# Exponentials of a decoder stack: 32x32 block transposes on VectorE and moves by DMA in place of TensorE transposes

## The reference, cut to what matters

```python
x = x + att0                    # attention 0: batch 0 alone, one result added to all batches
x = mamba_block(x)              # projection, causal 4-tap convolution, scan over 8 heads, gate
x = x + cross_attention(ln(x))  # attention 1: 8 heads of 32, padding mask
x = ln(x + mha_causal(x))       # attention 2: 16 heads of 16
x = ln(x + mha(x, context))     # attention 3: 16 heads of 16
x = ln(x + fc2(relu(fc1(x))))
x = ln(x + mha_causal(x, ctx))  # attention 4: 16 heads of 16
x = x + down(gelu(up(x)))
```

## Time and profile before

| what | us |
|---|---|
| median of 3 runs | 1736.97 |
| lowest, highest run | 1736.25, 1737.17 |
| span of the profiled execution | 1734.3 |
| TensorE busy in it | 1664.1 |
| ScalarE busy | 1357.1 |
| VectorE busy | 1313.4 |
| GpSimd busy | 533.5 |

### The profile page before, as it was taken

One profiled execution on the slowest core, in us unless ns is written; L12 is line 12 of the kernel. 1 busy time (PEld: TensorE's weight loads), 2 busy tenths in 40 slices (PEclk: granted clock), 3 DMA queues, 4 the chain that ended last, 5 costly groups with the idle time before them and its releaser, 6 DMA issues.

```text
span 1734.3 us, 54906 instructions
## 1 busy us (share of the span) xinstructions
PE 1664.1 (96%) x21232; PEld 1438.0 (83%) x21232; DVE 1313.4 (76%) x3355; ACT 1357.1 (78%) x4026; POOL 533.5 (31%) x1288
## 2 busy tenths in 40 slices
PE   6789999999999999999999999999999999999976
PEld 6577888888888888888888888888888888888765
DVE  3577778887778888877888887788888778888542
ACT  2367888888888888888888888888888888888763
POOL 1333233332323333232333333233333323333110
PEclk9899999999999999999999999999999999999998
DMA  7000000000000000000000000000000000000000
GB/s 266 8 8 8 8 8 12 6 10 9 11 12 11 11 6 10 9 11 11 12 11 8 8 8 11 12 11 11 10 5 9 10 11 11 9 5 5 5 4 10
DMA packets 26176, 26.92 MB, mean 16 GB/s; under 512 B 2240, under 2 KB 25024, under 8 KB 25792
## 3 DMA queue, kind: packets, MB, share of 16 engines
q1 hardware_dynamic: 25920, 23.41, 4.1%
HBM read 19.21 MB, written 4.19 MB: 13 GB/s over the span
## 4 chain that ended last, share of the span: by engine, by line
PE 88%; DVE 7%; issue 2%; ACT 1%; POOL 1%; DMA 0%; DVEq 0%; SPq 0%; POOLq 0%; ACTq 0%
PE ring L581 26%; PE ring L587 22%; PE ring L569 18%; PE score L637 6%; PE ring L678 5%; PE ring L755 3%; PE ring L765 2%; DVE conv L1237 2%; PE ring L668 2%; PE ring L816 1%; DVE conv L1231 1%; PE score L628 1%; DVE neg_max L1144 1%; PE ring L748 1%; ACT exps L954 1%
## 5 line engine op out<-in xcount | busy, mean ns | idle before, releaser
L954 ACT ACTIVATE exps<-score,neg_max 128x128 f32<-128x128 f32 x1808 | 491.4, 409 | 112.7 <-DVE neg_max L1144 112.7
L1144 DVE TENSOR_REDUCE neg_max<-score 128x4 f32<-128x512 f32 x452 | 289.8, 683 | 118.9 <-PE score L637 118.8
L1400 POOL TENSOR_TENSOR stat<-stat 128x1 f32<-128x1 f32 x224 | 128.8, 575 | 698.3 <-DVE stat L1116 698.3
L960 ACT COPY weights<-ring 128x512 f32<-128x512 f32 x452 | 257.3, 658 | 44.0 <-PE ring L569 42.3
L569 PE MATMUL ring<-const,exps 128*128 128x128 f32 x1808 | 240.1, 275 | 11.6 <-ACT exps L954 7.9
L569 PEld LDWEIGHTS ring<-const,exps 128*128 128x128 f32 x1808 | 210.2, 142 | 33.9 <-ACT exps L954 15.8
L1231 DVE SCALAR_TENSOR_TENSOR conv<-raw,vectors,conv 128x128 f32<-128x128 f32 x576 | 168.5, 348 | 6.8
L581 PE MATMUL ring<-actT,w_q 128*128 128x128 f32 x1024 | 138.0, 278 | 2.5 <-ACT actT L926 2.5
L637 PE MATMUL score<-K,QB 32*128 32x128 f32 x3616 | 135.2, 283 | 0.5 <-issue 0.5
L637 PEld LDWEIGHTS score<-K,QB 32*128 32x128 f32 x3616 | 113.8, 188 | 21.9 <-issue 21.7
L926 ACT COPY actT<-ring 128x256 f32<-128x256 f32 x224 | 86.4, 386 | 56.3 <-PE ring L569 56.3
(11 more groups left out here) (165 smaller groups left out, 3472.5 us busy)
## 6 DMA issues: line engine op xcount, KB each, us to landing
cT<-in_ctxT SPq DMA_DIRECT2D x32, 128.0 KB, 2.1
x_in<-in_x SPq DMA_DIRECT2D x32, 128.0 KB, 2.0
out<-result SPq DMA_DIRECT2D x32, 128.0 KB, 2.1
row_all<-in_rows SPq DMA_DIRECT2D x1, 1420.0 KB, 10.2
w_in<-in_in_proj SPq DMA_DIRECT2D x1, 1288.0 KB, 7.2
w_k<-in_k SPq DMA_DIRECT2D x4, 256.0 KB, 6.1
w_v<-in_v SPq DMA_DIRECT2D x4, 256.0 KB, 6.3
w_q<-in_q SPq DMA_DIRECT2D x4, 256.0 KB, 6.8
```

Source lines behind the costliest of these rows:

```text
L954: last = run(exps[:, n, h * P:(h + 1) * P], of, ACT.Exp, bias=neg_max[:, m, h:h + 1])
L960: nc.scalar.copy(weights[:, buffer(it, a_, l, t, WEIGHT_BUFFERS), half * 4 * P:(half + 1) * 4 * P], t_[:, :]).then_inc(read, 1)
L1144: nc.vector.tensor_reduce(neg_max[:, m, 4 * half:4 * half + 4].rearrange("p (b h) -> p b h", b=each), score[:, first:first + each, 0:4 // ...
L1400: tt(stat[:, l, 10:11], stat[:, l, 2:3], stat[:, l, 4:5], ALU.pow).then_inc(S[done], 1)
```

## The change

- No transpose of exponentials is on TensorE any more (BY_PE is empty). ScalarE writes the exponentials of a part in blocks: 4 blocks of (8 heads x 32 keys). One VectorE instruction transposes all 32x32 blocks of the part's 128x1024 in place (`turn_blocks`). Then SP issues 4 DMAs of 128 KB, SBUF to SBUF, one for each quarter of the query partitions; each spreads 32 partitions x 4 runs of 1 KB over 128 partitions of `weights` (`move_blocks`). TensorE's `values` waits for the landing and reads the weights with a stride pattern.
- Column 32 b + i of the scores lands on partition 4 i + b of the weights. So that V can stay as it is, that column holds key 4 i + b: keys, masks and the causal constant are stored in this order, for which ScalarE and VectorE read the key projections from PSUM with a stride of 4 elements.
- `exps` has 3 buffers and not 2. An exponential waits for the move of the part three before; a move waits for the flip and for the reader of the part four before.
- Attention 1's sums come from the exponentials' accumulators; VectorE inverts 8 columns, and TensorE spreads them with as many matmuls as had `ones`. ScalarE copies the outputs (`crossed`) and VectorE multiplies.
- From VectorE to ScalarE: the last tap of the convolution (from PSUM, six Identity activations), xhat, and the row tests (Abs with an accumulator) after x2T and x3T. From VectorE to GpSimd: x1, the gate's product, the additions of epsilon, and the comparisons with zero.
- K1 and V1 have 2 buffers and not 4. The tables TASKS, FIRST, LAST, SETUP and SHIFT are all new; PERIOD is still 14. In the new tables TensorE's list near the third attention reads e3, values1, back4, n3, xbc1, Wo, z0, x2T, x6T, Q2, values3, and VectorE's scores3_1, softplus, turn3_0, down, e3, turn3_1, finish1, finish4, n3, Wo.
- In setup, matmuls that only keep TensorE running stand at other tasks (SPARE), nine of them before values0.

```diff
+BY_PE = ()
 PERIOD = 14
 SCORE_BANKS = 4
-EXPS_BUFFERS = 2
+EXPS_BUFFERS = 3
 MAXIMA_BUFFERS = 4
 WEIGHT_BUFFERS = 4
+BLOCK = P // TILES
...
+            def move_blocks(it, a_, l, t):
+
+                n, _ = turned(it, a_, l, t)
+                part_of = exps[:, buffer(it, a_, l, t, EXPS_BUFFERS), :]
+                sp.wait_ge(S["flipped"], flipped(it, a_, l, t))
+                old = slot_before(it, a_, l, t, WEIGHT_BUFFERS)
+                if old is not None:
+                    was_a, _, was_l, was_i = old
+                    b, use = job(Of(was_i), f"values{was_a}", was_l)
+                    sp.wait_ge(bank_read[b], use + 1)
+                for q, rows_of in enumerate(ROWS_OF):
+                    sp.dma_start(weights[:, n, q * 2 * P:(q + 1) * 2 * P],
+                                 part_of[rows_of].rearrange("i (b x) -> i b x", b=TILES)).then_inc(S[f"turned{n}"], 16)
...
-                    for at, summed in ((D, True), (0, False)):
-                        for c in range(DC):
-                            for r in range(TILES):
-                                h = TILES * c + r
-                                last = mm(output[ROWS_OF[r], at + c * P:at + (c + 1) * P], ones[:, :] if summed else V1[:, l, h, :],
-                                          exps_of(0, heads_of(1, 0).index(h)), start=True, stop=True)
-                                if not summed and c == DC - 1:
-                                    last.then_inc(full if r == TILES - 1 else S[f"att_full{r}"], 1)
+                    pe.wait_ge(S["shares"], nth(it, l))
+                    for c in range(DC):
+                        for r in range(TILES):
+                            h = heads_of(1, 0).index(TILES * c + r)
+                            mm(output[ROWS_OF[r], D + c * P:D + (c + 1) * P], shares[:, l % 2, h:h + 1].broadcast_to((P, DH8)), ident,
+                               start=True, stop=True)
+                    for c in range(DC):
+                        for r in range(TILES):
+                            h = TILES * c + r
+                            last = mm(output[ROWS_OF[r], c * P:(c + 1) * P], V1[:, l % 2, h, :],
+                                      exps_of(0, heads_of(1, 0).index(h)), start=True, stop=True)
+                            if c == DC - 1:
+                                last.then_inc(full if r == TILES - 1 else S[f"att_full{r}"], 1)
...
+                into = exps[:, n, :].rearrange("p (h i b) -> p h b i", h=HEADS, b=TILES) if (a_, t) in BY_PE else exps[
+                    :, n, :].rearrange("p (b h i) -> p h b i", b=TILES, h=HEADS)
+                old = slot_before(it, a_, l, t, EXPS_BUFFERS)
+                if old in STREAMED:
+                    was_a, was_t, was_l, was_i = old
+                    moved, count = turned(Of(was_i), was_a, was_l, was_t)
+                    act.wait_ge(S[f"turned{moved}"], count)
                 for half in range(HALVES):
                     act.wait_ge(S["maxima"], part(it, a_, l, t) * HALVES + half + 1)
                     for h in range(4 * half, 4 * half + 4):
                         of = score[:, 4 * t + h // 2, h % 2 * P:(h % 2 + 1) * P] if a_ == 1 else score[
                             :, 2 * t + h // 4, h % 4 * P:(h % 4 + 1) * P]
-                        last = run(exps[:, n, h * P:(h + 1) * P], of, ACT.Exp, bias=neg_max[:, m, h:h + 1])
+                        if a_ == 1:
+                            last = run(into[:, h], by_block(of), ACT.Exp, bias=neg_max[:, m, h:h + 1], accum_out=sums[:, l % 2, h:h + 1])
+                        else:
+                            last = run(into[:, h], by_block(of), ACT.Exp, bias=neg_max[:, m, h:h + 1])
...
+            def crossed(it, l):
+
+                for r in range(TILES - 1):
+                    act.wait_ge(S[f"att_full{r}"], nth_output(it, 1, l))
+                t, _ = filled(it, "values1", l)
+                nc.scalar.copy(actT[:, l, :, :].rearrange("p c k -> p (c k)"), t[:, 0:D]).then_inc(S["crossed"], 1)
...
+            def xhat(it, l):
+                act.wait_ge(S["rstd1"], nth(it, l))
+                run(att[:, l, :], res[:, l, :], ACT.Copy, scale=stat[:, l, 10:11]).then_inc(S["xhat"], 1)
...
+                               t[:, 0:n * P].rearrange("p (c k) -> p c k", c=n))
+                for k in range(n):
+                    c = half * n + k
+                    last = run(conv[:, l % 2, c, :], t[:, k * P:(k + 1) * P], ACT.Identity,
+                               scale=conv_w[:, c, TAPS - 1:TAPS], bias=conv_b[:, c:c + 1])
+                last.then_inc(read, 1)
...
+            def nonzero_rows(it, what, l, mask, done):
+
+                act.wait_ge(bank_full[job(it, what, l)[0]], job(it, what, l)[1] + 1)
+                run(att[:, l, :], res[:, l, :], ACT.Abs, accum_out=mask[:, l, 0:1]).then_inc(S[done], 1)
+
+            def x2T(it, l):
+                copy_out(it, "x2T", l, actT[:, l], D)
+                nonzero_rows(it, "x2T", l, mask0, "sum0")
+
+            def x3T(it, l):
+                copy_out(it, "x3T", l, actT[:, l], D)
+                nonzero_rows(it, "x3T", l, mask1, "sum1")
...
+            def keys_out(it, what, lane):
+
+                t, read = filled(it, what, lane)
+                for c in range(DC):
+                    last = nc.scalar.copy(by_block(K2[:, lane, c, :]), in_blocks(t[:, c * P:(c + 1) * P]))
+                last.then_inc(read, 1)
...
+            def turn_blocks(it, a_, l, t):
+
+                part_of = exps[:, buffer(it, a_, l, t, EXPS_BUFFERS), :]
+                dve.wait_ge(S["exps"], (part(it, a_, l, t) + 1) * HALVES)
+                nc.vector.transpose(part_of, part_of).then_inc(S["flipped"], 1)
+                if a_ == 1:
+                    nc.vector.reciprocal(shares[:, l % 2, :], sums[:, l % 2, :]).then_inc(S["shares"], 1)
...
-                    for c in chunks:
-                        last = ts(conv[:, l % 2, c, :], raw[:, l % 2, c, TAPS - 1:], conv_w[:, c, TAPS - 1:TAPS],
-                                  conv_b[:, c:c + 1], ALU.mult, ALU.add)
                     for k in range(TAPS - 1):
-                        step(last)
+                        if k:
+                            step(last)
...
+                    heads_out = actT[:, l, :, :].rearrange("p c k -> p (c k)")
+                    tt(heads_out, heads_out, t[:, D:], ALU.mult).then_inc(read, 1)
...
+            def root(it, l, step, seed, done, src=1, scale=1.0, offset=EPS):

                 wait_for(S[seed], nth(it, l))
+                step(ts(stat[:, l, 2:3], stat[:, l, src:src + 1], scale, offset, ALU.mult, ALU.add))
...
+                def x1(l):
+
+                    wait_for(S[f"x_in{l % 2}"], nth_of_two(it, l) * 16)
+                    if it.iteration > 0:
+                        b, use = job(Of(it.iteration - 1), "x6T", l)
+                        wait_for(bank_full[b], use + 1)
+                        wait_for(S["plus"], nth(Of(it.iteration - 1), l))
+                    elif l == 0:
+                        evacuated(it, "back0", 0)
+                    tt(res[:, l, :], x_in[:, l % 2, :], att0[:, :], ALU.add).then_inc(S["x1"], 1)
+
+                def gate(l):
+
+                    wait_for(S["gated"], nth(it, l))
+                    evacuated(it, "Y", l)
+                    m = l % 2
+                    tt(zs[:, m, :], tz[:, m, :], zs[:, m, :], ALU.mult).then_inc(S["u"], 1)
```

More of the change, by code:

```diff
@@ L50 @@
 TASKS = dict(
-    loadx=-39.297, loadc=-21.957, x1=-31.388, x1r=0.609, xhat=34.036, xhatT=-8.817, dt=1.27, softplus=-2.884, am=-12.308,
-    xbc0=-7.003, xbc1=-5.859, z1=-5.461, z0=1.147, K1=-7.656, V1=-0.645, conv0=10.153, conv1=1.914, silu=8.942, pairs=2.154,
-    ld=3.18, decayed=4.453, Y=4.486, uT=5.016, proj=5.731, xnT=7.896, Q1=8.272, finish1=10.278, Wo=13.01, x2T=13.36, K2=15.065,
-    Q2=13.819, V2=18.506, e2=15.211, n2=15.74, finish2=23.561, norm2=19.381, x3T=23.838, row=23.91, K3=24.14, Q3=25.27, V3=24.234,
@@ new lines @@
+    loadx=103.7121, loadc=21.4043, x1=116.7214, x1r=-23.4055, xhat=45.2037, xhatT=101.7706, dt=99.7564, softplus=95.7542,
+    am=54.033, xbc0=104.3449, xbc1=108.5224, z1=106.1759, z0=109.068, K1=104.7433, V1=113.8264, conv0=-120.7388, conv1=-135.3793,
+    silu=69.6664, pairs=112.0066, ld=112.9754, decayed=-70.1916, Y=113.9575, uT=116.0593, proj=116.6788, xnT=118.0147,
+    Q1=118.7217, finish1=121.3722, Wo=123.0545, x2T=123.0968, K2=124.3273, Q2=123.6151, V2=127.245, e2=128.1891, n2=129.6912,
@@ new lines @@
+    finish2=126.3402, norm2=107.8796, x3T=133.292, row=133.8575, K3=133.9645, Q3=133.9878, V3=133.4515, e3=135.9867, n3=136.7537,
+    finish3=218.343, norm3=203.3623, x4T=139.2029, fc1=140.5645, fc2=141.5169, norm4=112.8326, K4=142.6938, V4=146.2533,
+    x5T=143.3817, Q4=144.4216, finish4=178.2296, norm5=189.3358, x6T=151.5575, up0=152.8902, up1=153.0532, down=163.2307,
+    store=263.3565, quads1=119.0754, scores1_0=142.4452, turn1_0=160.0378, values1=122.0848, quads2=125.979, scores2_0=207.3992,
@@ L196 @@
```

(22 more changed lines are left out.)

446 lines of the change are left out of this document (256 added, 190 removed), and 2 rows, old and new, of the table S.

## The result

The changed kernel takes 1855.07 us (median of 4 runs, 1851.48 to 1859.87) against 1736.77 us (1736.25 to 1737.17) for the kernel before beside it: a ratio of 1.068, with a 95% interval of 1.0662 to 1.0698. I had forecast 1588, 9% faster; it is 7% slower.

The account below looks back on a forecast made before the run. TensorE was taken as the only steady bound, busy 96% of 1734.3 us. 1734.3 - 197 (transposes) + 38 (waits) + 10 (setup, drain) = 1585 us of span, 1588 as a run; range 1545 to 1625, chance 0.58.

Parts of the forecast that it names:

- So in the steady part TensorE is the only bound: Steady batches of 50.53 us: TensorE busy 50.33, with ScalarE (83%) and VectorE (81%) running in its shadow.
- What the cover costs: Waits when VectorE is busy 41.9 of 44.4 us: 1.2 us a batch, 38 us; setup and drain add 10 us.
- Rival 3: The change frees nothing: waits refill the time taken off TensorE exactly, 1737 us within 3.5; chance 0.02.
- Rival 1: In-order queues bind: waits of 2.5 to 6 us a batch from late moves or slower VectorE transposes, 1630 to 1733; chance 0.24.
- Rival 2: VectorE takes TensorE's place, slower kernel: a block transpose of 2.5 us or more gives 1754 us or more; chance 0.09.
- Part 1: Transposes taken off TensorE: 226 parts at 0.87 us, 197 us in all, 6.1 us a batch, all on the path.
- Part 2: ScalarE's load: ring copies go (8.0 us a batch), new work adds 7.5; from 42.05 to 41.5 us a batch.
- above 63: Sign of being wrong: table loads above 63; ScalarE would reach 42.8 us with one more in each batch.
- Part 3: VectorE's load: 7.8 us a batch goes, seven block transposes at 1.23 us come; 41.9 us a batch.
- Part 4: GpSimd's load: the gate, x1 and some ten one-column operations add 4.3 us, to 20.8 of 44.4; no bound.
- Part 5: Moves into weights, 904 transfers of 128 KB: 3.7 us from flip to landing; over 5, TensorE waits once a batch.
- The queue: SP's DMA queue: packets took 4.1% of 16 engines' span; the moves add 21% of a 1537 us span; no bound.

Follow-up runs that it names:

- e7: Changed kernel with no turning: ScalarE writes exponentials straight into weights, with no VectorE transposes and no moves; order and small work kept; 1771.33 us, ratio 1.0191.
- e8: Kernel before with no turning: without its 1808 TensorE transposes, ScalarE's 452 copies and 14 spare setup matmuls; own order and small work; 1771.19 us, ratio 1.0191.
- e1: Changed kernel without the moves: VectorE's block transpose writes straight into weights, all else kept; 1803.03 us, ratio 1.037 to the kernel before.
- e9: e8 with other places in each engine's order for some tasks, same work; 1640.67 us, ratio 0.9428 to the kernel before.
- e3: Changed kernel with only the gate's product moved back from GpSimd to VectorE; 1855.36 us, ratio 1.0675 to the kernel before.
- e4: e3 plus the additions of epsilon back on VectorE for five of a batch's seven powers; 1849.22 us, ratio 1.0662 to the kernel before.
- e5: Changed kernel, same instructions, with other places in each engine's order for some tasks; 1898.29 us, ratio 1.0919 to the kernel before.
- e10: Changed kernel, same instructions, with a second new order after e5; 1869.2 us, ratio 1.0748 to the kernel before.
- e12: e8 with 16 more matmuls a batch whose result nobody reads, from the fifth batch on; 1758.01 us, ratio 1.0121 to the kernel before.

## Why the prediction was wrong

**What it comes to.** The steps from the changed kernel back:

| kernel | us | step |
|---|---|---|
| before | 1737 | |
| e7: new order and small work, no turning | 1771 | +34 |
| e1: with VectorE's transposes | 1803 | +32 |
| changed kernel: with the moves | 1855 | +52 |

The first step is the one that matters: with the turning gone altogether, neither kernel's own order (e7, e8) goes below 1771. Of the 267 us between my 1588 and the 1855 measured, 183 are there in e7. TensorE's largest wait, for the last step of a norm, is there too: 92.5 us in e7, 105.7 in e1, 90.4 in the changed kernel. That e7 and e8 come to the same time is no sign of one cause: e7's chain is 40% TensorE, 25% ScalarE and 22% VectorE, where e8's is 41% VectorE.

**The step that failed: "So in the steady part TensorE is the only bound", with ScalarE and VectorE "in its shadow".** I read this from 503.64 busy of 505.5 us and a chain of 88% TensorE. Both were true and neither says what comes next. A chain names one path; a second one through VectorE, of nearly the same length, was hidden by it. e8 shows it for the kernel before: all the transposes that I priced at 197 us were taken out, and the time did not fall; e9 shows that it was the order, 130 us less with the same work. The Trainium skill (Perfetto Trace Analysis, Identifying the Most-Contended Engine) warns that matmul busy share is no good measure of how close TensorE is to its roofline. No run here measures a roofline. What this case adds is that the share doesn't price a removal either: it fell from 96% to 85% in e8, and the span is 32 us longer.

**"What the cover costs", 1.2 us of waits a batch,** is that error as a term of the sum. I bounded the waits by VectorE's mean idle time, 9.7 us a batch. The idle time isn't spread: 3.7 of the 9.7 lie before the maxima, and between 925 and 940 us VectorE idled 1.0 us where its mean would be 2.9, which the stretches of 5 us in the profile of before show. Measured: a batch of 53.5 us with TensorE busy about 46.1 (436.01 / 505.5 x 53.5), so 7.4 us of waits. The batch has 3.0 us more than the 50.53 of the earlier trace rows; the forecast wanted 4.9 less.

**Rival 3, "the change frees nothing", had 0.02, as "nothing in the profile is for it".** For its first half that was wrong: e8 frees nothing. Rival 1 had the right mechanism for the rest (cross waits of in-order queues, late moves), but I capped it at today's time, as if TensorE's work were all that could bind (its own upper end, 6 us a batch, gives 1550 + 192 = 1742 and not the 1733 that I wrote). Rival 2, the one on the slower side, rested on a slow transpose and that isn't what happened.

**Term by term.**
- Part 1, 197 us off TensorE: its busy time fell by 109 us in the changed kernel and by 157 in e8, where transposes and 14 spare matmuls went. The matmuls that stayed take longer (L581 with `w_q`: 278 ns in the mean before, 288 in e8). The lower clock (0.968 in the mean, 0.988 before) is one possible reason, less overlap between waits another; they weren't separated.
- Part 2, ScalarE 41.5 us a batch: 368.80 / 505.5 x 53.5 = 39.0. There are 64 table loads, two a batch, as assumed. My sign of being wrong, "above 63", was badly set: the kernel before has 64 too.
- Part 3, the block transpose: 1.23 forecast, 1.235 measured, 226 times. The row for 1024 columns of the earlier trace rows was the right neighbour. The Trainium skill (VectorE: DVE Perf Modes, The three transpose paths) has 311 ns for 128x128 of bf16; scaled by columns, an estimate, that gave 2.5 us, and the trace shows half of it for this shape. The Trainium skill (Vector Engine (DVE) Microarchitecture Reference, 3.8) says that the reorder array sustains one element per cycle and lane; the trace agrees in that the transpose takes as long as the product of as many elements, 1226 ns. VectorE a batch: 41.9 forecast, 407.55 / 505.5 x 53.5 = 43.1 measured. But priced "in the shadow" the transposes cost nothing, and they cost 32 us (e7 to e1).
- Part 4, GpSimd 20.8: 206.00 / 505.5 x 53.5 = 21.8. No bound, as said; e3 and e4 agree.
- Part 5, a move of 3.7 us: 5.4 from the end of the flip to the landing, and 7.9 from the end of the first flip to the second landing where two parts are in the queue (983.69 to 991.56). The issue was priced by a load (0.38); a move's is 0.60, one every 0.65 us, and a landing takes 2.7 where I took 2.1. I had written that over 5 us TensorE waits there once a batch; it waits for them 49.5 us in all at L811 and 14.4 at L796, and leaving them out gives 52 us (e1). One such move in the changed kernel's chain, in order of time:

```profile
925.40 1.16 DVE exps L1329
926.58 0.54 SPq L646
927.17 0.60 SPq L646
927.81 0.60 SPq L646
928.46 3.49 DMA weights<-exps
932.19 0.64 PE ring L796 x16
```

- The queue: 21% forecast for the moves alone. The 33.0% measured hold the loads and stores too, which were 4.1% before, so the moves are some 29%. It hid no bound.
- Two signs of being wrong that I had named came true: moves over 5 us with TensorE waiting, and a clock below 1.00 in the middle (0.99 from 300 to 805.5 us).

**What stays open.** What holds e7, the changed kernel's own order without turning, at 1771 wasn't taken apart task by task; that it is a second chain as in e8 is argued from the like, and not shown. That an order exists in which the changed kernel beats 1737 is neither shown nor excluded: e9 gained 130 us by order alone, but without turning, and the two tries with it (e5, e10) lost. Turning only some parts on VectorE and the rest on TensorE wasn't tried, as it needs an order of its own. No version that computes the reference was faster than the kernel before.

## What to carry to other kernels

A chain that is 88% one engine says what ends last, not by how much. Before pricing work off it, take that work out altogether (e8: one kernel) and see whether the time falls. Failing that, look for stretches of a few microseconds in which a second engine is nearly as full as the first; they are a warning and not a proof. And a kernel whose order is fixed by hand can be tied to its durations: here less work in the old order was a longer time (e8), and the same less work in another order a shorter one (e9).

## What the runs showed of the hardware

- A block transpose of 128x1024 float32 on VectorE takes 1235 ns, as long as a product of the same size (1226).
- A move from SBUF to SBUF on SP's queue is issued in 0.60 us (median of 904), against 0.38 for a load from HBM. The kind of transfer isn't all of it: with the moves in the queue the loads of `cT` are issued in 0.545 us and the stores in 0.597 (medians, changed kernel), without them in 0.378 and 0.344 (e1). While moves run, the loads of `cT` land 2.6 us after their issue and not 2.1.
- VectorE is slowed by GpSimd. L1309 has two inputs in SBUF and takes 483 ns at least and 742 in the mean, up to 1408; the gate on GpSimd takes 1314. With the gate back on VectorE (e3) its mean is 547 and its maximum 869. One of the long ones, beside the gate's product (start, us):

```profile
903.73 1.31 POOL L1640 TENSOR_TENSOR zs<-tz,zs 128x512 f32<-128x512 f32 x1
903.96 1.37 DVE L1309 SCALAR_TENSOR_TENSOR res<-att,stat,row_all 128x256 f32<-128x256 f32 x1
```

  The Trainium skill (GPSIMD Engine Reference, 1. Specifications) says that the two share their SBUF interfaces and that VectorE's instructions with two SBUF inputs contend for them; these rows agree. Here it cost little: e3 gained nothing, e4 6 us.
- More work made a kernel faster: 16 matmuls a batch that nobody reads, 13 us (e12), with the granted clock up from 0.968 to 0.981.
